# A cross-attention step with its two halves exchanged: values first, then the keys of one step further ahead

## The chip, the cores and the metric

The kernel runs on one core of a Trainium2 chip. The metric is the device time of one execution in microseconds (us), here the median of the runs of the kernel. A profiled execution gives the trace from which the rows below are read.

## The reference, cut to what matters

The program is one layer of a perceiver: cross-attention of 128 latent rows to a context of 12544 rows, then linear attention, causal attention and a mixture of eight experts on the 128 rows. Nearly all the time, and all of the change, is in the cross-attention:

```python
q = layernorm(x) @ Wq.T + bq                 # 128 x 256, 16 heads of 16
k = ctx @ Wk.T + bk                          # 12544 x 256
v = ctx @ Wv.T + bv                          # 12544 x 256
scores = einsum('bhqd,bhkd->bhqk', q * 0.25, k)
attn = softmax(scores, axis=-1)
x = x + einsum('bhqk,bhkd->bhqd', attn, v).reshape(...) @ Wo.T + bo
```

All of it is float32. The kernel keeps the accuracy by splitting operands into a high part and a low part in a float32r form and multiplying three of the four combinations.

## The kernel before, in words

**Tiling.** The 12544 context rows are cut into 49 pieces (`NS`) of 256 rows (`SK`). Four pieces make a block (`BS`), so there are 13 blocks. The program is a loop over steps t = 0 to 55. In one step, different pieces are at different stages:

- piece t+2: its keys (`keys`, 12 matmuls into `k_bank`, PSUM bank 0) and its values (`values`, 12 matmuls into `v_bank`, bank 1);
- piece t: the running maxima (`max_scores`: 16 matmuls, read by VectorE's `step_max`);
- piece n = t - 5 (`LAG`): the scores (`scores`, 16 matmuls, with the block's maxima subtracted by two extra rows of the query matrix `qmat`) and their exponentials on ScalarE (`exponential`);
- piece n - 1: the weighted values, a burst of 64 short matmuls (`weighted_values`, L605 in the trace) that accumulate in `pv_bank`.

**A step.** A step has eight slots, q = 0 to 7. In each slot TensorE does two matmuls of scores (L589), two of maxima (L565) and three of keys or values: keys (L533) in slots 0 to 3, values (L548) in slots 4 to 7. The burst comes at the end of slot 1. The maxima go to two banks in turn, so `max_scores` of a slot waits until VectorE has read that of two slots earlier (`mx_read`).

**Key parts.** Keys leave PSUM twice: ScalarE writes the high part to `kst` with the bias added (`keys_high`, L371, two instructions), VectorE the low part (`keys_low`, L901, two instructions). Before the change ScalarE does so after the exponential of slot 4 and VectorE after the maximum of slot 5. Then SyncE issues six DMAs (`keys_place`, L242) that copy `kst` to `kT`, a ring of 7 pieces, in the layout that the scores need. SyncE waits for three things before them: the low parts, a POOL memset of the ring slot (only for the first seven pieces), and the scores of the piece whose ring slot is overwritten. That is piece n-7, whose scores are done at the end of step n-2, the step in which the parts of piece n leave PSUM. TensorE waits for the six DMAs of piece t at the start of step t (`keys_placed`).

**Values out.** The values leave PSUM in one copy (`values_out`), by ScalarE for the first pieces and by VectorE (L911) from piece 6 on, in slot 1 of the following step.

**Context parts.** ScalarE makes the high part of the context of piece t+3 in slot 1 (`context_high`, L361), POOL then makes the low part (`context_low`, L314), both into a ring of two buffers, `cparts`. `ctx_load` on SyncE fetches the context of piece t+6 at the start of step t.

**Turned maxima.** After the last step of a block (in step last+1), VectorE reduces the maxima of four pieces (`block_max`, L925 to L935), TensorE turns them by a transpose in slot 2 (`turn_max`, L574, into `v_bank`), VectorE copies the result (`max_turned`, L942) and SyncE sends it to `qmat` by two DMAs (`max_rows`, L255). The scores of that block start at step last+2 and wait for these DMAs.

**Before and after the loop.** Ahead of step 0 come the keys and values of pieces 0 and 1. Steps 0 to 4 have no scores and no burst. From step 47 on there are no keys and no values, from step 49 on no maxima.

All order is written out by hand: each engine runs its own list, and semaphores connect them. There is no planner.

Of the kernel before, what the change touches and what calls it, by code (L numbers as in the profile page):

```python
# [6 lines left out]
F32R = mybir.dt.float32r  # L7
# [5 lines left out]
P = 128  # L13
# [8 lines left out]
NS = KEYS // SK  # L22
BS = 4
NB = (NS + BS - 1) // BS
LAG = BS + 1
# [31 lines left out]
def last_step(b):  # L57
    return min(b * BS + BS, NS) - 1
# [46 lines left out]
def perceiver_layer(nc, dr, out):  # L105
    ctx = ExitStack()
    with ctx:
# [3 lines left out]
        S = {n: ctx.enter_context(nc.semaphore(n)) for n in COUNTING + ONCE + LOADS + ["dve_chain"]}  # L111
# [18 lines left out]
        maxparts = sb("maxparts", [P, 8, 2, PAIRS], F32R)  # L130
        maxT = sb("maxT", [32, P], F32R)
# [223 lines left out]
        def _(act):  # L355
            def context_high(n):

                act.wait_ge(S[f"ld_ctx{n % CRING}"], 16 * (n // CRING) + 16)
                if n >= 2:
                    act.wait_ge(S["v_done"], 2 * (n - 2) + 2)  # L360
                act.activation(cparts[n % 2][:, 0, :, :], ctxT[n % CRING][:, :, :], ACT.Copy  # L361
                               ).then_inc(S["ch_ready"], 1)
# [12 lines left out]
            def values_out(n):  # L375


                act.wait_ge(S["v_done"], 2 * n + 2)
                if n >= VRING:
                    act.wait_ge(S["pv_done"], 2 * (n - VRING) + 2)  # L380
                act.activation(val[:, n % VRING, :, :, 0:HD].rearrange("p j h d -> p (j h) d"),  # L381
                               v_bank[:, :].rearrange("p (g d) -> p g d", d=HD), ACT.Copy).then_inc(S["val_ready"], 1)
# [32 lines left out]
            last.then_inc(S["act_q0"], 1)  # L415
            values_out(0)
            context_high(2)
            for t in range(LAST + 2):
                for q in range(8):
                    n = t - LAG  # L420
                    if 0 <= n < NS:
                        exponential(n, q)
                    if q == 1 and 0 <= t + 1 <= LAG:
                        values_out(t + 1)
                    if q == 1 and t + 3 < NS:
                        context_high(t + 3)
                    if q == 2:
                        for b in range(NB):
                            if n - 1 == last_step(b):
                                part_out(b)  # L430
                    if q == 4 and t + 2 < NS:
                        keys_high(t + 2)
                    if t == NS + 1 and q == 2:

                        act.wait_ge(S["dve_dmax"], 1)
                        act.activation(bmax[:, :, :], bmax[:, :, :], ACT.Exp).then_inc(S["act_bw"], 1)
# [71 lines left out]
        def _(pe):  # L508
# [16 lines left out]
            def keys(n, t, half):  # L525

                if (t, half) == (0, 0):
                    pe.wait_ge(S["cl_ready"], n + 1)
                    if n == 1:
                        pe.wait_ge(S["kl_ready"], 1)  # L530
                for i in range(3 * half, 3 * half + 3):
                    pw, pc, c = products[i]
                    last = pe.matmul(k_bank[:, t * SK:(t + 1) * SK], wk[:, pw, c, t * P:(t + 1) * P], cparts[n % 2][:, pc, c, :],  # L533
                                     start=(i == 0), stop=(i == 5))
                if (t, half) == (1, 1):
                    last.then_inc(S["k_done"], 1)

            def values(n, j, half):

                if (j, half) == (0, 0) and n >= 1:  # L540
                    turned = [b for b in range(NB) if last_step(b) == n - 3]
                    if turned:
                        pe.wait_ge(S["mt_read"], turned[0] + 1)
                    else:
                        pe.wait_ge(S["val_ready"], n)
                for i in range(3 * half, 3 * half + 3):
                    pw, pc, c = products[i]
                    last = pe.matmul(v_bank[:, j * D:(j + 1) * D], cparts[n % 2][:, pc, c, j * P:(j + 1) * P], wv[:, pw, c, :],  # L548
                                     start=(i == 0), stop=(i == 5))
                if half == 1:  # L550
                    last.then_inc(S["v_done"], 1)
# [5 lines left out]
            def max_scores(n, p):  # L557

                m = 8 * n + p
                if m >= 2:  # L560
                    pe.wait_ge(S["mx_read"], m - 1)
                for a in range(2):
                    if p == 0 and a == 1 and 0 < n + 2 < NS:
                        pe.wait_ge(S["kl_ready"], n + 2)
                    last = pe.matmul(mx_bank[p % 2][:, a * SK:(a + 1) * SK], qM[:, p, a, :], kT[:, n % RING, p, :],  # L565
                                     start=True, stop=True)
                last.then_inc(S["mx_done"], 1)

            def turn_max(b):


                pe.wait_ge(S["mparts_ready"], 2 * b + 2)
                pe.wait_ge(S["val_ready"], min(last_step(b) + 3, NS))
                pe.transpose(v_bank[:, 0:P].bitcast(F32R), maxparts[:, :, :, :].rearrange("q a s p -> q (a s p)"),  # L574
                             ident_r[:, :]).then_inc(S["mt_done"], 1)

            def scores(n, q):
# [37 lines left out]
            def turn_part(b):  # L615

                pe.wait_ge(S["part_ready"], b + 1)
                if b == 0:
                    pe.wait_ge(S["ld_small"], 64)
                    pe.wait_ge(S["kl_ready"], NS)  # L620
                if b == 1:
                    pe.wait_ge(S["mt_read"], NB)
                if b >= 2:
                    pe.wait_ge(S["dve_partT_read"], b - 1)
                for g in range(GROUPS):
                    last = pe.matmul(B[b % 2][:, g * GH * VW:(g + 1) * GH * VW], parts[:, b, g * P:(g + 1) * P],  # L626
                                     const[:, C_SEL:C_SEL + GH * VW], start=True, stop=True)
                last.then_inc(S["pe_partT"], 1)
# [32 lines left out]
            for n in range(2):  # L661
                for j in range(2):
                    for half in range(2):
                        values(n, j, half)
            pe.wait_ge(S["dve_q0"], 1)
            pe.wait_ge(S["act_q0"], 1)
            for t in range(LAST + 2):
                n = t - LAG
                for q in range(8):
                    if q == 0 and n < 0:  # L670
                        keys_placed(t)
                    if 0 <= n < NS:
                        scores(n, q)
                    if t < NS:
                        max_scores(t, q)
                    if q == 2:
                        for b in range(NB):
                            if t == last_step(b) + 1:
                                turn_max(b)
                    if t + 2 < NS:  # L680
                        if q < 4:
                            keys(t + 2, q // 2, q % 2)
                        else:
                            values(t + 2, (q - 4) // 2, q % 2)
                    if q == 1 and 0 <= n - 1:
                        weighted_values(n - 1, 0)
                        weighted_values(n - 1, 1)
                    if t > NS and q % 4 == 3 and 2 * (t - NS - 1) + q // 4 < NB - 3:
                        turn_part(2 * (t - NS - 1) + q // 4)
            for b in range(NB - 3, NB):  # L690
                turn_part(b)
# [155 lines left out]
        def _(dve):  # L847
# [89 lines left out]
            def max_turned(b):  # L937

                dve.wait_ge(S["mt_done"], b + 1)
                if b >= 1:  # L940
                    dve.wait_ge(S["max_rows"], 32 * b)
                dve.tensor_copy(maxT[:, :], v_bank[0:32, 0:P]).then_inc(S["mt_read"], 1)  # L942


            dve.memset(warm[:, :], 0.0).then_inc(S["dve_warm"], 1)
# [27 lines left out]
            for t in range(LAST + 2):  # L973
                for b in range(NB):
                    if t == last_step(b) + 1:
                        block_max(b)
                for q in range(8):
                    if t < NS:
                        step_max(t, q)
                    if q == 1 and LAG < t + 1 < NS:  # L980
                        values_out(t + 1)
                    if q == 2:
                        for b in range(NB):
                            if t == last_step(b) + 1:
                                max_turned(b)
                    if q == 5 and t + 2 < NS:
                        keys_low(t + 2)


            dve.wait_ge(S["ld_small"], 64)  # L990
# [283 lines left out]
```

## Time and profile before

| | us |
|---|---|
| median of 3 runs | 589.88 |
| lowest, highest | 588.37, 593.8 |
| the profiled execution | 590.74 |
| span of its trace | 588.9 |
| PE busy in the span | 555.1 (94%) |
| DVE busy | 423.2 (72%) |
| ACT busy | 331.6 (56%) |
| DMA queue q1, share of 16 engines | 64.1% |

A row of the trace names a line of the kernel, an engine and an operation. PE is a matmul on TensorE, PEld a weight load, DVE VectorE, ACT ScalarE, POOL GpSimd, SPq the DMA issue of SyncE. Matmuls overlap each other, so that their own durations are longer than the distance from one to the next; the chain of work shows that distance. The granted clock (PEclk) is a share of full speed: 1.00 is 2.4 GHz, 0.50 is 1.2 GHz.

### The profile page before, as it was taken

The numbers are of one execution on the slowest core, as the hardware profiler recorded it, in microseconds if no ns is written. First come the engines' busy times: TensorE is split into PE (matmuls) and PEld (weight loads), VectorE is DVE, ScalarE is ACT, GpSimd is POOL, SyncE is SP. The second block draws the span as 40 slices with busy tenths as digits, with TensorE's granted clock in tenths as the row PEclk, the third lists the DMA queues.
The fourth block names the chain that finished last, engine by engine and source line by source line (L and its number), as shares of the span: only waits on it lengthen the run. The fifth ranks groups of instructions, "written<-read, shape, count | busy, mean of one in ns | idle before, by whom it ended". The sixth has DMA issues, their size and how long they took to land.

```text
span 588.9 us, 15872 instructions
## 1 busy us (share of the span) xinstructions
PE 555.1 (94%) x6517; PEld 512.9 (87%) x6517; DVE 423.2 (72%) x804; ACT 331.6 (56%) x636; POOL 91.5 (16%) x75
## 2 busy tenths in 40 slices
PE   7778999999999999999999999999998998878797
PEld 7677899999999999999999999999986887846686
DVE  5678787787787787777787877877875237876674
ACT  3322666576676676676666666766766650052463
POOL 7551111111101101101101111011000000006000
PEclk9888999999999999999999999999999999988899
DMA  5999887768768778768678687785375009920000
GB/s 183 135 144 143 144 192 114 126 119 120 121 118 124 117 116 127 117 111 128 119 113 128 118 117 120 118 126 98 78 110 170 3 27 376 375 82 1 1 0 9
DMA packets 44651, 70.46 MB, mean 120 GB/s; under 512 B 6788, under 2 KB 15140, under 8 KB 44452
## 3 DMA queue, kind: packets, MB, share of 16 engines
q1 hardware_dynamic: 44580, 69.47, 64.1%
q8 instruction: 50, 0.82, 0.8%
q14 instruction: 21, 0.17, 0.1%
HBM read 30.56 MB, written 0.13 MB: 52 GB/s over the span
## 4 chain that ended last, share of the span: by engine, by line
PE 79%; DVE 7%; DMA 7%; SPq 3%; ACT 2%; issue 2%; DVEq 0%; ACTq 0%
PE bank L589 16%; PE bank L605 15%; PE bank L565 15%; PE bank L533 11%; PE bank L548 10%; DMA kT<-kst 5%; PE bank L805 3%; SPq L242 3%; PE bank L821 2%; PE bank L613 1%; DMA ctxT<-in_ctxT 1%; PE bank L626 1%; DVE stepmax L917 1%; DMA qmat<-maxT 1%; PE bank L518 1%
## 5 line engine op out<-in xcount | busy, mean ns | idle before, releaser
L917 DVE TENSOR_REDUCE stepmax<-bank 128x2 f32<-128x512 f32 x392 | 263.4, 688 | 98.8 <-PE bank L565 76.3
L391 ACT ACTIVATE probs<-bank 128x512 f32<-128x512 f32 x392 | 226.9, 602 | 146.3 <-PE bank L589 144.9
L565 PE MATMUL bank<-kT,qM 128*128 128x256 f32 x784 | 166.3, 294 | 8.5 <-DMA kT<-kst 7.1
L589 PE MATMUL bank<-qmat,kT 128*128 128x256 f32 x784 | 162.8, 292 | 4.3 <-DMA kT<-kst 1.7
L589 PEld LDWEIGHTS bank<-qmat,kT 128*128 128x128 f32 x784 | 120.2, 191 | 17.6 <-issue 10.1
L565 PEld LDWEIGHTS bank<-kT,qM 128*128 128x128 f32 x784 | 123.0, 194 | 14.2 <-DMA kT<-kst 7.0
L314 POOL TENSOR_TENSOR cparts<-ctxT,cparts 128x512 fp32r<-128x512 f32 x49 | 62.7, 1279 | 338.4 <-ACT cparts L361 338.4
L533 PE MATMUL bank<-cparts,wk 128*128 128x256 f32 x588 | 104.2, 288 | 1.9 <-DVE kst L901 1.9
L548 PE MATMUL bank<-wv,cparts 128*128 128x256 f32 x588 | 101.9, 284 | 0.7 <-ACT val L381 0.7
L605 PE MATMUL bank<-probs,val 128*17 128x128 f32 x3136 | 95.1, 273 | 0.0
L533 PEld LDWEIGHTS bank<-cparts,wk 128*128 128x128 f32 x588 | 86.2, 196 | 2.3 <-POOL cparts L314 2.3
L605 PEld LDWEIGHTS bank<-probs,val 128*17 128x17 f32 x3136 | 81.4, 97 | 6.5
L548 PEld LDWEIGHTS bank<-wv,cparts 128*128 128x128 f32 x588 | 84.6, 193 | 0.9 <-ACT val L381 0.9
L371 ACT ACTIVATE kst<-bank,kbias 128x256 fp32r<-128x256 f32 x98 | 40.9, 472 | 22.1 <-PE bank L533 22.1
L901 DVE SCALAR_TENSOR_TENSOR kst<-bank,kbias,kst 128x256 fp32r<-128x256 f32 x98 | 42.5, 475 | 4.1 <-ACT kst L371 4.1
L361 ACT ACTIVATE cparts<-ctxT 128x512 fp32r<-128x512 f32 x49 | 30.5, 623 | 3.5 <-DMA ctxT<-in_ctxT 3.5
L911 DVE COPY val<-bank 128x512 f32<-128x512 f32 x43 | 29.2, 680 | 0.0
L350 POOL TENSOR_TENSOR low<-w,high 128x512 fp32r<-128x512 f32 x8 | 10.1, 1303 | 109.7 <-ACT high L462 109.7
L805 PE MATMUL bank<-high,tparts 128*128 128x512 f32 x64 | 20.2, 439 | 0.2 <-DVE tparts L1142 0.2
L1181 DVE TENSOR_TENSOR low<-w,high 128x1024 f32 (+1 forms) x12 | 14.7, 1222 | 6.0 <-ACT high L462 6.0
L613 PE MATMUL bank<-const 128*128 128x128 f32 x136 | 18.9, 285 | 0.0
L613 PEld LDWEIGHTS bank<-const 128*128 128x128 f32 x136 | 17.8, 201 | 0.3
(188 smaller groups left out, 324.9 us busy)
## 6 DMA issues: line engine op xcount, KB each, us to landing
kT<-kst SPq DMA_DIRECT2D x294, 128.0 KB, 4.6
ctxT<-in_ctxT SPq DMA_DIRECT2D x49, 256.0 KB, 5.3
w<-in_w SPq DMA_DIRECT2D x24, 512.0 KB, 10.1
bias<-in_biases SPq DMA_DIRECT2D x1, 1024.0 KB, 5.9
qmat<-maxT SPq DMA_DIRECT2D x26, 8.0 KB
w_xk<-in_w_xk SPq DMA_DIRECT2D x1, 256.0 KB, 3.4
w_xq<-in_w_xq SPq DMA_DIRECT2D x1, 256.0 KB, 3.5
bias<-in_biases SPq DMA_DIRECT2D x1, 256.0 KB, 6.0
```

The lines of the kernel that those rows point to most:

```text
L314: pool.tensor_tensor(cparts[n % 2][:, 1, :, :], ctxT[n % CRING][:, :, :], cparts[n % 2][:, 0, :, :].bitcast(F32), ALU.subtract).then_inc(S ...
L371: last = act.activation(kst[n % 2][:, 0, t * SK:(t + 1) * SK], k_bank[:, t * SK:(t + 1) * SK], ACT.Identity, bias=kbias[:, t:t + 1])
L391: act.activation(probs[k % PROBS][:, :, :], sc_bank[k % 3][:, :].rearrange("p (h q) -> p h q", q=P), ACT.Exp).then_inc(S["exp_ready"], 1)
L533: last = pe.matmul(k_bank[:, t * SK:(t + 1) * SK], wk[:, pw, c, t * P:(t + 1) * P], cparts[n % 2][:, pc, c, :], start=(i == 0), stop=(i == 5))
L548: last = pe.matmul(v_bank[:, j * D:(j + 1) * D], cparts[n % 2][:, pc, c, j * P:(j + 1) * P], wv[:, pw, c, :], start=(i == 0), stop=(i == 5))
L565: last = pe.matmul(mx_bank[p % 2][:, a * SK:(a + 1) * SK], qM[:, p, a, :], kT[:, n % RING, p, :], start=True, stop=True)
L589: last = pe.matmul(sc_bank[k % 3][:, i * 2 * P:(i + 1) * 2 * P], kT[:, n % RING, p, j * P:(j + 1) * P], qmat[b % 2][:, p, :, :], start=Tru ...
L605: last = pe.matmul(pv_bank[32 * r:32 * r + VW, g * P:(g + 1) * P], val[:, n % VRING, j, GH * g + r, :], probs[(GROUPS * ch + g) % PROBS][: ...
L613: pe.matmul(B[6][:, 0:P], ident, ident, start=True, stop=True)
L805: last = pe.matmul(B[2 * which + i][:, :], tparts[:, a, c, :], weights, start=(n == 0), stop=(n == len(products) - 1))
L901: last = dve.scalar_tensor_tensor(kst[n % 2][:, 1, cols], k_bank[:, cols], kbias[:, t:t + 1], kst[n % 2][:, 0, cols].bitcast(F32), ALU.add ...
L917: dve.tensor_reduce(stepmax[:, n % BS, 2 * p:2 * p + 2], mx_bank[p % 2][:, :].rearrange("p (a k) -> p a k", a=2), AX_X, ALU.max).then_inc( ...
```

## The change

The two halves of a step are exchanged. Values of piece t+2 are computed in slots 0 to 3, and keys of piece t+3 (not t+2) in slots 4 to 7. The keys of piece 2 move ahead of the loop. The key parts of piece t+2, whose matmuls now lie in the step before, leave PSUM in step t in slot 0 on ScalarE and slot 1 on VectorE, beside the burst. The values leave in slot 5 of the same step instead of slot 1 of the next. The context's high part is made in slot 5, of piece t+4. The turned maxima use `k_bank` instead of `v_bank`, because that bank is now the one that is empty in slot 2. The waits follow: TensorE's wait for the context parts moves to slot 2, the wait for the key parts to slot 4, and the wait for the values out of PSUM to slot 0. No instruction that computes or copies is added or taken away, and the ring sizes stay.

```diff
@@ ScalarE: before the loop, and in the loop
             values_out(0)
             context_high(2)
+            values_out(1)
+            context_high(3)
             for t in range(LAST + 2):
                 for q in range(8):
                     n = t - LAG
                     if 0 <= n < NS:
                         exponential(n, q)
-                    if q == 1 and 0 <= t + 1 <= LAG:
-                        values_out(t + 1)
-                    if q == 1 and t + 3 < NS:
-                        context_high(t + 3)
+                    if q == 0 and t + 2 < NS:
+                        keys_high(t + 2)
+                    if q == 5 and t + 2 <= LAG:
+                        values_out(t + 2)
+                    if q == 5 and t + 4 < NS:
+                        context_high(t + 4)
...
-                    if q == 4 and t + 2 < NS:
-                        keys_high(t + 2)
@@ TensorE: keys, values, max_scores, turn_max, turn_part
             def keys(n, t, half):
 
                 if (t, half) == (0, 0):
-                    pe.wait_ge(S["cl_ready"], n + 1)
-                    if n == 1:
-                        pe.wait_ge(S["kl_ready"], 1)
+                    if n < 3:
+                        pe.wait_ge(S["cl_ready"], n + 1)
+                    if n >= 1:
+                        turned = [b for b in range(NB) if last_step(b) == n - 4]
+                        if turned:
+                            pe.wait_ge(S["mt_read"], turned[0] + 1)
+                        else:
+                            pe.wait_ge(S["kl_ready"], n)
...
                 if (j, half) == (0, 0) and n >= 1:
-                    turned = [b for b in range(NB) if last_step(b) == n - 3]
-                    if turned:
-                        pe.wait_ge(S["mt_read"], turned[0] + 1)
-                    else:
-                        pe.wait_ge(S["val_ready"], n)
+                    pe.wait_ge(S["val_ready"], n)
...
-                    if p == 0 and a == 1 and 0 < n + 2 < NS:
-                        pe.wait_ge(S["kl_ready"], n + 2)
+                    if p == 2 and a == 1 and n + 3 < NS:
+                        pe.wait_ge(S["cl_ready"], n + 4)
...
                 pe.wait_ge(S["mparts_ready"], 2 * b + 2)
-                pe.wait_ge(S["val_ready"], min(last_step(b) + 3, NS))
-                pe.transpose(v_bank[:, 0:P].bitcast(F32R), maxparts[:, :, :, :].rearrange("q a s p -> q (a s p)"),
+                pe.wait_ge(S["kl_ready"], min(last_step(b) + 4, NS))
+                pe.transpose(k_bank[:, 0:P].bitcast(F32R), maxparts[:, :, :, :].rearrange("q a s p -> q (a s p)"),
@@ TensorE: before the loop, and in the loop
+            for t in range(2):
+                for half in range(2):
+                    keys(2, t, half)
...
-                    if t + 2 < NS:
-                        if q < 4:
-                            keys(t + 2, q // 2, q % 2)
-                        else:
-                            values(t + 2, (q - 4) // 2, q % 2)
+                    if q < 4 and t + 2 < NS:
+                        values(t + 2, q // 2, q % 2)
+                    if q >= 4 and t + 3 < NS:
+                        keys(t + 3, (q - 4) // 2, q % 2)
@@ VectorE: max_turned, and in the loop
-                dve.tensor_copy(maxT[:, :], v_bank[0:32, 0:P]).then_inc(S["mt_read"], 1)
+                dve.tensor_copy(maxT[:, :], k_bank[0:32, 0:P]).then_inc(S["mt_read"], 1)
...
-                    if q == 1 and LAG < t + 1 < NS:
-                        values_out(t + 1)
+                    if q == 1 and t + 2 < NS:
+                        keys_low(t + 2)
...
-                    if q == 5 and t + 2 < NS:
-                        keys_low(t + 2)
+                    if q == 5 and LAG < t + 2 < NS:
+                        values_out(t + 2)
```

**VectorE's list around a block's end.** The names: `stepmax` is the maximum of one slot, `kst` the low key parts, `val` the copy of the values, `curmax` to `bmax` the block's maxima, `maxT` the copy of the turned ones. Before:

```order
L917 TENSOR_REDUCE stepmax<-bank 128x2 x4
L901 SCALAR_TENSOR_TENSOR kst_75<-bank,kbias,kst_75 128x256 x2
L917 TENSOR_REDUCE stepmax<-bank 128x2 x2
L925 TENSOR_REDUCE curmax<-stepmax 128x16
L931 TENSOR_SCALAR maxparts<-curmax 128x2x8
L933 SCALAR_TENSOR_TENSOR maxparts<-curmax,maxparts 128x2x8
L935 TENSOR_SCALAR bmax<-curmax 128x16
L917 TENSOR_REDUCE stepmax<-bank 128x2 x2
L911 COPY val<-bank 128x32x16
L917 TENSOR_REDUCE stepmax<-bank 128x2
L942 CAST maxT<-bank 32x128
L917 TENSOR_REDUCE stepmax<-bank 128x2 x3
```

With the change:

```order
L923 TENSOR_REDUCE stepmax<-bank 128x2 x4
L917 COPY val<-bank 128x32x16
L923 TENSOR_REDUCE stepmax<-bank 128x2 x2
L931 TENSOR_REDUCE curmax<-stepmax 128x16
L937 TENSOR_SCALAR maxparts<-curmax 128x2x8
L939 SCALAR_TENSOR_TENSOR maxparts<-curmax,maxparts 128x2x8
L941 TENSOR_SCALAR bmax<-curmax 128x16
L923 TENSOR_REDUCE stepmax<-bank 128x2 x2
L907 SCALAR_TENSOR_TENSOR kst_74<-bank,kbias,kst_74 128x256 x2
L923 TENSOR_REDUCE stepmax<-bank 128x2
L948 CAST maxT<-bank 32x128
L923 TENSOR_REDUCE stepmax<-bank 128x2 x3
```

The two key instructions and the one value copy have changed places: the copy stands after slot 5 and the keys after slot 1.

**TensorE's list from slot 7 of a step over slots 0 and 1 of the next.** `qmat,kT` are scores, `kT,qM` maxima, `cparts,wk` keys, `wv,cparts` values; in brackets are the semaphores waited for. Before:

```order
L548 MATMUL bank<-wv,cparts_70 128x256 x3
L589 MATMUL bank<-qmat_51,kT 128x256 [waits exp_ready]
L589 MATMUL bank<-qmat_51,kT 128x256 [waits kt_load1]
L565 MATMUL bank<-kT,qM 128x256 [waits mx_read]
L565 MATMUL bank<-kT,qM 128x256 [waits kl_ready]
L533 MATMUL bank<-cparts_71,wk 128x256 [waits cl_ready]
L533 MATMUL bank<-cparts_71,wk 128x256 x2
```

With the change:

```order
L540 MATMUL bank<-cparts_71,wk 128x256 x3
L592 MATMUL bank<-qmat_51,kT 128x256 [waits exp_ready]
L592 MATMUL bank<-qmat_51,kT 128x256 [waits kt_load1]
L568 MATMUL bank<-kT,qM 128x256 [waits mx_read]
L568 MATMUL bank<-kT,qM 128x256
L551 MATMUL bank<-wv,cparts_71 128x256 [waits val_ready]
L551 MATMUL bank<-wv,cparts_71 128x256 x2
```

Slot 0 now has values where it had keys, and one wait less; the wait for `mx_read` in front of the maxima is unchanged.

## Rows read from the trace of the kernel before

**Rows 1.** Page: engines' shares of the chain that ended last.

```profile
PE 79%; DVE 7%; DMA 7%; SPq 3%; ACT 2%; issue 2%; DVEq 0%; ACTq 0%
```

**Rows 2.** Chain of waits, slots 7 to 1 of a middle step: start us, us, what.

```profile
239.04 1.87 PE bank L605 x64
...
246.14 0.24 PE bank L589 x2
246.38 0.39 PE bank L565 x2
246.77 0.36 PE bank L533 x3
...
247.37 0.24 PE bank L565 x2
...
247.96 1.87 PE bank L605 x64
```

**Rows 3.** Timeline of the same place: start, us, engine, line, operation.

```profile
244.75 0.87 DVE L901 SCALAR_TENSOR_TENSOR kst<-bank,kbias,kst 128x256 fp32r<-128x256 f32 x2
...
245.53 2.81 DVE L917 TENSOR_REDUCE stepmax<-bank 128x2 f32<-128x512 f32 x4
...
245.64 3.77 SPq L242 DMA_DIRECT2D kT<-kst  x6
...
246.26 0.50 PE L565 MATMUL bank<-kT,qM 128*128 128x256 f32 x2
...
248.25 0.68 DVE L911 COPY val<-bank 128x512 f32<-128x512 f32 x1
```

**Rows 4.** Chain of waits from step 0 to step 6.

```profile
22.02 0.47 PE bank L565 x2
...
27.70 0.79 DVE kst L901 x2
28.51 0.55 SPq L242
...
31.67 5.23 DMA kT<-kst
...
36.94 0.80 PE bank L565 x2
...
67.15 0.38 PE bank L589
```

**Rows 5.** Timeline around the starts of steps 0, 1 and 5; in brackets idle time before.

```profile
22.02 0.47 PE L565 MATMUL bank<-kT,qM 128*128 128x256 f32 x2 [2.14 <-DMA kT<-kst]
...
28.40 5.20 DVE L917 TENSOR_REDUCE stepmax<-bank 128x2 f32<-128x512 f32 x8
...
29.23 0.47 PE L565 MATMUL bank<-kT,qM 128*128 128x256 f32 x2 [0.62 <-DVE stepmax L917]
...
29.84 1.29 POOL L314 TENSOR_TENSOR cparts<-ctxT,cparts 128x512 fp32r<-128x512 f32 x1 [3.26 <-ACT cparts L361]
...
59.62 0.50 PE L589 MATMUL bank<-qmat,kT 128*128 128x256 f32 x2 [0.85 <-DMA qmat<-maxT]
```

**Rows 6.** Stretches: us, busy (x) of PE PEld DVE ACT POOL, PEclk, DMA share, GB/s.

```profile
24.00:26.00 2.00, 2.00 (x11) 2.00 (x10) 1.30 (x2) 0.00 (x0) 2.00 (x2) 0.50 1.09 137
...
28.00:30.00 2.00, 1.38 (x12) 1.21 (x11) 1.94 (x5) 1.12 (x2) 0.16 (x1) 1.00 0.12 40
30.00:43.00 13.00, 10.57 (x74) 10.26 (x73) 10.05 (x18) 2.80 (x6) 7.72 (x5) 0.87 1.05 148
```

**Rows 7.** `stepmax` instructions while a POOL instruction on the context runs: count, duration ns min/median/max.

```profile
L917 DVE TENSOR_REDUCE stepmax<-bank x3: 681/690/691, 29.7 to 31.0; 128x2 f32<-128x512 f32 x3
```

**Rows 8.** Chain of waits, steps 46 to 48.

```profile
433.08 0.79 DVE kst L901 x2
...
437.05 5.65 DMA kT<-kst
```

**Rows 9.** Chain of waits at the start of step 37.

```profile
341.59 3.22 DMA qmat<-maxT
```

More of the change, by code:

```diff
@@ L620, in turn_part @@
                     pe.wait_ge(S["kl_ready"], NS)
+                    pe.wait_ge(S["mt_read"], NB)
                 if b == 1:
-                    pe.wait_ge(S["mt_read"], NB)
+                    pe.wait_ge(S["val_ready"], NS)
                 if b >= 2:
```

## The prediction

> **What bounds the kernel now.** I read the page first: 79% of the chain that ended last is TensorE, and DMA only 7% [rows 1]. The chain in order of time then shows two regimes. In the middle it is TensorE without a gap that the page counts as idle. From one burst to the next are 247.96 - 239.04 = 8.92 us [rows 2], and steps 6 to 46 all look like that. Two matmuls take 0.24 us there, three take 0.36. Only one place in a step is longer for no visible reason: the two maxima of slot 0 take 0.39 where those of slot 1 take 0.24. The timeline explains it [rows 3]. VectorE starts the low key parts at 244.75, after the maximum of slot 5, and needs 0.87. The maximum of slot 6 can start only at 245.53 and, at 0.69 us, is read by 246.22. TensorE's slot 0 of the next step writes the same bank, and it starts at 246.26, right behind that. Without the extra 0.15 of the chain (0.39 against 0.24) it would have started at about 246.11. So 0.15 us of each step is a wait for VectorE that is too short to appear as idle time.
>
> In the start-up it is different. From step 0 at 22.02 to step 6 at 67.15 two steps take about 15 us (the first two 36.94 - 22.02 = 14.9, [rows 4]), though TensorE's 40 matmuls of a step need 40 x 0.12 = 4.8 us. The loop that sets this pace is: start of step t, key parts in slots 4 and 5 (27.70 + 0.79), six DMA issues from 28.51 on [rows 4], the last landing at 31.67 + 5.23 = 36.90, start of step t+2.
>
> **The change, part by part.** The sum is made against the profiled execution, 590.74 us, which is 0.86 above the median of the three runs.
>
> *Steady steps.* VectorE's work per step is the same: eight maxima, 0.87 of keys, 0.68 of values [rows 3]. The keys now follow slot 1, where VectorE waits for TensorE through the 1.87 us of the burst [rows 2]; 0.87 fits and costs nothing. Before, the values' 0.68 stood there. The values now follow slot 5. There they delay the maximum of slot 6 by 0.68 where the keys did so by 0.87, so it is read 0.19 earlier, at 246.03 in the times of rows 3. TensorE's own pace asks for 246.11, so the stall of 0.15 goes, with some 0.04 to spare after the 0.04 of signalling. What is late next is nothing on VectorE: slot 7 follows by 0.69 where TensorE allows 0.84. I found the same 0.39 in some 30 of the 40 steps 7 to 46 and 0.27 to 0.36 in those next to a block's end, so 30 x 0.15 + 10 x 0.09 = **5.4 us**.
>
> ScalarE and POOL only change the hour. The high key parts (ScalarE, slot 0) delay the exponential of slot 1, which the burst hides; without the burst it would be 0.8 us against 0.24 us of spare per slot. The context goes high and low in slots 5 to 7, two slots or more ahead of TensorE's wait in slot 2. SyncE's six key DMAs of a middle step are issued at 245.64, the moment the low parts are done, but they also wait for the scores of slot 7, which end within 0.2 us of that. So earlier key parts do not make these DMAs earlier: no gain, no loss. Moving waits on TensorE costs nothing either: the three keys of slot 0 stand behind a wait for `cl_ready` and take 0.36 [rows 2], like any other three.
>
> *Start-up.* With the keys of piece 2 ahead of the loop, the low parts leave after two maxima, about 2.8 us into step 0, not at 27.70 (5.7 in). The 12 matmuls moved ahead, 1.4 us, fall in TensorE's wait of 2.14 us for the first DMAs [rows 5]: nothing. The latency loop becomes 2.8, six issues of 3.8 in all [rows 3] and a landing of 5.2 [rows 4], 11.8 us for two steps. Two other things are slower than that. VectorE needs 5.20 for eight maxima [rows 5] and 0.87, so 6.1 a step. The DMA engines are full: 13 us with a share of 1.05 carried two steps' keys and contexts [rows 6], so 6.5 a step. Step 1 starts at 29.23 as before [rows 5], since its keys are untouched; step 6 then starts at 29.2 + 5 x 6.5 = 61.7 by DMA. By VectorE it is 29.5 + 5 x 6.1 plus block 0's reduction (0.7), its copy (0.3) and two value copies (1.4) = 62.4. Before it was 67.15. So at most 4.8 is gained. Against it stand step 5's wait for the turned maxima of block 0, queued behind a full set of key DMAs (59.62, [rows 5]), and TensorE's clock, granted at 0.50 after each long wait [rows 6]. Steps of 7.0 instead of 6.5 would leave 2. I take **4.0 us**, nearer the upper end, because the waits that lower the clock get shorter.
>
> *End.* Step 46 has only values now: 12 x 0.12 = 1.44 us less. The keys of piece 48 wait for the end of that step's scores as much as for their own low parts (433.08 + 0.79), and step 48 starts when they land at 437.05 + 5.65 = 442.7 [rows 8]. All of that moves ahead by 1.44. Step 47 may now wait up to 1 us for piece 47, but piece 48's DMAs do not wait for it. I take **1.4 us**.
>
> *Turned maxima.* TensorE's transpose at a block's end needs the low key parts out of `k_bank`. VectorE starts the block's reduction about 0.9 us into the step and needs 0.7 for it, 1.3 for two maxima and 0.87 for the keys, 3.8 in all; the transpose comes after three slots and the burst, 3 x 0.84 + 1.87 = 4.4. So 0.6 is to spare, where the values had 0.8. The DMAs that follow it landed too late for the next block once, at the start of step 37 (341.59 + 3.22, some 0.35 late) [rows 9]. With 0.15 less between the key DMAs and this one it may happen once more: **-0.3 us**.
>
> Sum: 5.4 + 4.0 + 1.4 - 0.3 = 10.5. 590.74 - 10.5 = 580.2, and 589.88 - 10.5 = **579.4 us** for the median.
>
> **The rivals.**
>
> *The stall in slot 0 stays (13%).* For it: my spare is 0.04 us, and slot 0 still has three waits on TensorE, so the 0.15 could belong to them rather than to VectorE. Against: TensorE's start is behind VectorE's end by 0.04 in every step that I looked at, and waits elsewhere cost nothing. Then only start-up and end gain: 589.88 - 5.1 = 584.8.
>
> *The maxima's DMAs are late at each block (8%).* Ten block ends lie in the steady part. If each costs the 0.35 of step 37, the sum falls by 3.2 more: 582.6.
>
> *POOL and VectorE collide (4%).* POOL's 1.3 us on the context [rows 5] used to run during the burst. Now it runs under the maxima of slots 6 and 7, where only 0.04 us is to spare. If a maximum had to wait for it, every step would lose up to 1.2, and 40 x 1.2 - 5.1 makes 633; the point from which the kernel is slower than before is a delay of 0.04 of spare, 0.15 and 5.1 / 40, together 0.32 us per step. Against it: three maxima took 681 to 691 ns while such a POOL instruction ran in step 1 [rows 5, 7], and 0.69 is also the time of one without it. The Trainium skill (SBUF — State Buffer, the section on the two sides of the memory) says that POOL and VectorE take an exclusive lock on a shared port pair when a VectorE instruction runs in a two-port mode or has two SBUF inputs, and that the loser waits for the whole instruction. By that rule a maximum, which reads PSUM, is not affected, and the trace agrees.
>
> *The exchange does not reach the start-up (5%).* If the full DMA engines already set the pace there, so that steps stay at 7.5, only 7 is left: 583.
>
> **How the numbers follow.** The forecast has 70%; its own range is 577.5 (start-up 4.8, stall 5.8, end 1.7) to 582.5 (start-up 2, stall 4.5, end 1). The rivals at 582.6 to 584.8 have 26%. The range 576.5 to 585 holds these less their outermost part. What a measurement of this kernel can tell from no change is about 1%, 5.9 us, so the line is at 584.0: faster by over 1% has 0.82 (the forecast, the two rivals below 584, less mishaps), within 1% 0.14, slower 0.04.
>
> **What would show it.** In the chain of a middle step the maxima of slot 0 take 0.24 and bursts are 8.78 apart. Step 6 starts near 63 and the share of DMA is above 1 through all of 30 to 60 us. Step 48 starts about 10.5 us earlier than at 442.7. I am wrong if the maxima of slot 0 stay at 0.39, if `stepmax` lasts over 0.7 us beside POOL, or if TensorE's idle time in front of L589 grows by releases from `maxT`.

## The result, and the profile after

The changed kernel takes 582.55 us in the median of 4 runs (581.65 to 583.93); the kernel before took 591.84 beside it (4 runs, 588.37 to 594.27). The ratio is 0.987, with a 95% interval of 0.982 to 0.991: 1.3% faster. In a second comparison, in 6 runs against 11, the same kernel gave 582.46 and a ratio of 0.983 (0.978 to 0.988). The forecast was 579.4 with a range of 576.5 to 585.0, and a gain of 10.5; by the two profiled executions the span shrank by 588.9 - 580.6 = 8.3.

The page of the changed kernel, against [rows 1]: the span, the granted clock in 40 slices, and the engines' shares of the chain.

```profile
span 580.6 us, 15874 instructions
...
PEclk9999999999999999999999999999999999988899
DMA  6999996766877877876768768777483029900000
...
PE 78%; DVE 10%; DMA 6%; SPq 3%; ACT 2%; issue 1%; DVEq 0%; ACTq 0%
```

**A middle step.** The chain of waits of the changed kernel, from slot 7 to the next burst, against [rows 2] (L568 are the maxima, L608 the burst). The maxima of slot 0, at 240.47, now take 0.24 like all others, and bursts are 8.78 apart.

```profile
239.63 0.24 PE bank L568 x2
240.47 0.24 PE bank L568 x2
241.31 0.24 PE bank L568 x2
241.91 1.87 PE bank L608 x64
...
250.69 1.87 PE bank L608 x64
```

The timeline of the same place, against [rows 3]: the values' copy stands where the keys stood, and it lets the next maximum start 0.60 later, where the keys took 0.78. POOL's context work now runs beside the maxima.

```profile
247.62 0.68 DVE L917 COPY val<-bank 128x512 f32<-128x512 f32 x1
247.96 1.29 POOL L314 TENSOR_TENSOR cparts<-ctxT,cparts 128x512 fp32r<-128x512 f32 x1 [7.49 <-ACT cparts L361]
248.22 0.68 DVE L923 TENSOR_REDUCE stepmax<-bank 128x2 f32<-128x512 f32 x1
```

How far TensorE had to wait is best seen on its weight loads (PEld), since the wait for the bank holds back the load of the maxima's weights too, and such a load runs 0.12 ahead of its matmul when nothing holds it (248.97 and 249.09 with the change). Before, the loads of scores and maxima at the start of slot 0, which stand 0.40 apart:

```profile
245.86 0.31 PEld L589 LDWEIGHTS bank<-qmat,kT 128*128 128x128 f32 x2
246.26 0.30 PEld L565 LDWEIGHTS bank<-kT,qM 128*128 128x128 f32 x2
```

With the change they stand 0.24 apart, as in every other slot, though only just: the maximum that frees the bank ends at 248.22 + 0.68 = 248.90, and the kernel before needed 0.05 from such an end (245.53 + 0.68 = 246.21) to the load at 246.26. That leaves 0.02.

```profile
248.73 0.31 PEld L592 LDWEIGHTS bank<-qmat,kT 128*128 128x128 f32 x2
248.97 0.31 PEld L568 LDWEIGHTS bank<-kT,qM 128*128 128x128 f32 x2
```

All `stepmax` instructions of 100 to 400 us, against [rows 7] (count, duration ns min/median/max): none is lengthened by POOL.

```profile
L923 DVE TENSOR_REDUCE stepmax<-bank x271: 678/691/693, 100.1 to 399.2; 128x2 f32<-128x512 f32 x136
```

**The start-up.** The chain of the changed kernel from step 1 to step 6, against [rows 4]. Step 1 starts at 28.20, step 3 at 41.16 (6.5 a step), step 6 at 61.52 instead of 67.15. From 43.77 to 54.60 the chain is nearly all VectorE; before it was six issues and a landing in each round. From 30.84 to 41.12 it still is, but the landing takes 7.12 instead of 5.23.

```profile
28.20 0.52 PE bank L568 x2
...
30.03 0.79 DVE kst L907 x2
...
34.00 7.12 DMA kT<-kst
...
41.16 0.52 PE bank L568 x2
...
42.99 0.78 DVE kst L907 x2
43.77 3.78 DVE stepmax L923 x6
...
49.54 0.79 DVE kst L907 x2
...
61.52 0.47 PE bank L592 x2
```

Two stretches of it (us, busy (x) of PE, PEld, DVE, ACT, POOL, PEclk, DMA share, GB/s), against [rows 6]. The clock stays at 1.00 where before it fell to 0.50 after each long wait, and the DMA engines have a mean share of 1.07 from 14 to 52 us, with no 2 us below 1.01. The prediction's sign, a share above 1 through all of 30 to 60 us, holds only to 52: from 52 to 62 it is 0.79.

```profile
30.00:43.00 13.00, 11.01 (x82) 10.06 (x82) 11.73 (x22) 3.91 (x8) 5.02 (x4) 1.00 1.07 164
14.00:52.00 38.00, 31.06 (x229) 28.28 (x230) 30.56 (x57) 12.95 (x27) 18.30 (x12) 1.00 1.07 158
```

**Step 8.** In the changed kernel one step has a wait that the kernel before does not have. The chain there: the six key DMAs of piece 8 are issued from 70.03 on, right behind 1.3 MB of biases and constants, and the last needs 7.73 us to land.

```profile
70.03 0.55 SPq L242
...
73.20 7.73 DMA kT<-kst
80.97 0.39 PE bank L592
```

**The end.** The chain of the changed kernel in step 46, against [rows 8]. Without keys in slots 4 to 7, TensorE waits for a maximum (422.96), and the scores of slot 7 release the DMA issue.

```profile
422.69 0.25 PE bank L568 x2
422.96 0.70 DVE stepmax L923
423.71 0.51 PE bank L568 x2
424.22 0.25 PE bank L592 x2
424.48 0.03 SPq L238
424.54 0.55 SPq L242
...
427.69 5.66 DMA kT<-kst
433.40 0.38 PE bank L592
```

The starts of the bursts (L605 before, L608 after), read from the timelines, make the account:

| burst of step | before | after | ahead by |
|---|---|---|---|
| 6 | 68.89 | 63.35 | 5.54 |
| 7 | 77.81 | 72.14 | 5.67 |
| 8 | 86.73 | 82.72 | 4.01 |
| 46 | 427.22 | 418.63 | 8.59 |
| 49 | 450.73 | 441.37 | 9.36 |
| 54, the last | 481.15 | 471.81 | 9.34 |
| end of the span | 588.9 | 580.6 | 8.3 |

Not all of this is the change. `e0_after` below is the changed kernel once more, and its bursts of steps 6 and 54 come 0.9 later than in the first profile. Nearly all of that is there already when step 0 starts, which moves with the first loads:

| profile | step 0 starts | last burst | between |
|---|---|---|---|
| kernel before | 22.02 | 481.15 | 459.13 |
| changed | 21.36 | 471.81 | 450.45 |
| `e0_after` | 22.34 | 472.74 | 450.40 |

In the seven other experiments step 0 starts at 21.50 to 22.47. So 0.66 of each line of the account lies in front of step 0 and is no gain that the change is shown to make; from step 0 to the last burst it makes 8.7.

### The profile page after: what moved, and what is told of

It is laid out like the page before. It is cut to its first block, busy times and chain, and to the rows that moved or that the text cites. A ratio compares the mean times of both kernels' runs of the same rounds, so it can differ in the third digit from the quotient of the medians.

```text
span 580.6 us, 15874 instructions
## 1 busy us (share of the span) xinstructions
PE 548.3 (94%) x6517; PEld 507.2 (87%) x6517; DVE 421.7 (73%) x804; ACT 331.4 (57%) x636; POOL 91.8 (16%) x75
## 4 chain that ended last, share of the span: by engine, by line
PE 78%; DVE 10%; DMA 6%; SPq 3%; ACT 2%; issue 1%; DVEq 0%; ACTq 0%
PE bank L592 17%; PE bank L608 15%; PE bank L568 14%; PE bank L551 10%; PE bank L540 10%; DMA kT<-kst 5%; PE bank L811 3%; PE bank L827 3%; SPq L242 2%; DVE stepmax L923 2%; PE bank L616 1%; PE bank L630 1%; DMA ctxT<-in_ctxT 1%; PE bank L520 1%; DVE kst L907 1%
## 5 line engine op out<-in xcount | busy, mean ns | idle before, releaser
L391 ACT ACTIVATE probs<-bank 128x512 f32<-128x512 f32 x392 | 230.8, 599 | 141.9 <-PE bank L592 137.5
L568 PE MATMUL bank<-kT,qM 128*128 128x256 f32 x784 | 161.1, 287 | 4.9 <-DMA kT<-kst 2.6
L568 PEld LDWEIGHTS bank<-kT,qM 128*128 128x128 f32 x784 | 121.4, 191 | 8.9 <-DVE stepmax L923 4.5
L540 PE MATMUL bank<-cparts,wk 128*128 128x256 f32 x588 | 101.1, 283 | 1.6 <-DVE kst L907 1.3
L608 PE MATMUL bank<-probs,val 128*17 128x128 f32 x3136 | 95.1, 273 | 0.0
L608 PEld LDWEIGHTS bank<-probs,val 128*17 128x17 f32 x3136 | 81.4, 97 | 6.5
L540 PEld LDWEIGHTS bank<-cparts,wk 128*128 128x128 f32 x588 | 83.8, 192 | 2.3 <-POOL cparts L314 2.1
```

Source lines behind the costliest of these rows:

```text
L391: act.activation(probs[k % PROBS][:, :, :], sc_bank[k % 3][:, :].rearrange("p (h q) -> p h q", q=P), ACT.Exp).then_inc(S["exp_ready"], 1)
L608: last = pe.matmul(pv_bank[32 * r:32 * r + VW, g * P:(g + 1) * P], val[:, n % VRING, j, GH * g + r, :], probs[(GROUPS * ch + g) % PROBS][: ...
```

## The experiments

Each was compared with the kernel before on the same chip. Since the part behind the last burst varies by itself (below), I read single terms from the bursts of the profiled execution.

**Is the stall of slot 0 VectorE's backlog?** Two experiments, one from each side. `e1_split` takes the kernel before and parts the low keys:

```diff
                     if q == 5 and t + 2 < NS:
-                        keys_low(t + 2)
+                        keys_low(t + 2, (0,))
+                    if q == 6 and t + 2 < NS:
+                        keys_low(t + 2, (1,))
```

(`keys_low` is given the halves that it shall do, and signals after the second.)

> The kernel before, with VectorE's two low-part instructions parted: one after slot 5, one after slot 6. Theory V (the 0.15 us of slot 0 is VectorE's backlog of 0.87 us on the maximum of slot 6): that maximum is now late by 0.43 only, so the maxima of slot 0 fall from 0.39 to 0.24; the maximum of slot 7 is late by both, so slot 1 should rise from 0.24 to about 0.30, and bursts be some 8.85 apart instead of 8.92. The start-up loop gets 0.7 longer each time, three times, step 6 near 69; the whole about 589 to 591 where before gives 591. Theory W (the 0.15 belongs to TensorE's three waits in slot 0): slot 0 stays at 0.39 and bursts at 8.92.

Measured: undisturbed bursts are 8.80 apart; slot 0 takes 0.27 instead of 0.39, and slot 1 stays at 0.24, not the 0.30 that I expected. Two rows of its chain, slots 0 and 1:

```profile
251.50 0.27 PE bank L565 x2
...
252.36 0.24 PE bank L565 x2
```

So theory V holds, and W falls: the three waits are all still there. But the kernel as a whole took 598.25, ratio 1.011 (1.004 to 1.019), some 7 us more than I expected. The timeline shows why:

```profile
250.85 0.47 DVE L901 SCALAR_TENSOR_TENSOR kst<-bank,kbias,kst 128x256 fp32r<-128x256 f32 x1
251.25 2.08 DVE L918 TENSOR_REDUCE stepmax<-bank 128x2 f32<-128x512 f32 x3
...
251.34 0.43 PE L565 MATMUL bank<-kT,qM 128*128 128x256 f32 x2
251.35 3.76 SPq L242 DMA_DIRECT2D kT<-kst  x6
```

The key DMAs start together with slot 0's maxima of the next step, where in the kernel before they start 0.6 ahead of them (245.64 against 246.26, [rows 3]). What SyncE issues behind them is late too, and the first steps of the blocks, steps 13 to 41, take 9.36 to 9.86 instead of 9.03 (9.39 once): eight waits for the turned maxima. The two waits for keys in the rows below are at step 8 (2.2) and in one middle step. The idle time in front of L589 from 68 to 430 us:

```profile
PE bank L589 <- DMA qmat<-maxT: 3.4, 8, 0.7
PE bank L589 <- DMA kT<-kst: 2.4, 2, 2.2
```

By the last burst (489.39 against 481.15) the loss is 8.2: 1.7 in the start-up, where I expected about 2, 2.2 in steps 7 and 8, 2.4 net in the steady part, and 1.9 in steps 47 to 49. That all of it comes from the later key DMAs is read from the timeline and was not tested by itself. The kernel before stood at two limits, with 0.15 to gain on one and hardly anything to give on the other.

`e2_dose` takes the changed kernel and lengthens the backlog after slot 5 with an instruction of no use:

```diff
                     if q == 5 and LAG < t + 2 < NS:
                         values_out(t + 2)
+                        dve.memset(small[:, 224:480], 0.0)
```

> The changed kernel, with one more VectorE instruction after the copy of the values in slot 5: it fills 256 unused columns and should take 0.2 to 0.33 us, so that the backlog on slot 6 is as large as the 0.87 of before or larger. Theory V: the wait comes back in slot 0, about this instruction's time less 0.06, so bursts are 8.92 to 9.05 apart instead of 8.78, and the kernel loses 40 times that, 6 to 11 us. Theory W: nothing moves, 582.5.

Measured: bursts 8.955 apart, and slot 0 at 0.43. The next maximum starts 251.28 - 250.41 = 0.87 behind the values' copy, where it was 0.60; it is 0.05 shorter than there, so it frees the bank 0.22 later. The loads of TensorE's maxima stand 0.44 behind those of the scores (251.53).

```profile
250.41 0.68 DVE L917 COPY val<-bank 128x512 f32<-128x512 f32 x1
251.10 0.27 DVE L994 MEMSET small<- 128x256 f32 x1
251.28 0.63 DVE L923 TENSOR_REDUCE stepmax<-bank 128x2 f32<-128x512 f32 x1
251.97 0.30 PEld L568 LDWEIGHTS bank<-kT,qM 128*128 128x128 f32 x2
```

A bank freed 0.22 later costs 8.955 - 8.78 = 0.175 a step: the spare is the rest, 0.05 at most, and the 0.04 of the forecast is of the right size. The last burst is 5.8 us later than in the changed kernel, of which 1.1 is a later start of step 0 (22.47). The other 4.6 are less than 40 x 0.175 = 7, because the longer step swallows all but one of the eight waits at block ends and most of that of step 8 (9.32 instead of 10.58). The whole took 586.23, ratio 0.990 (0.981 to 0.998). Theory V again.

**What sets the pace of the start-up now?** `e3_late` holds the key parts back by two slots there:

```diff
-                    if q == 0 and t + 2 < NS:
+                    if q == (2 if t < LAG else 0) and t + 2 < NS:
                         keys_high(t + 2)
...
-                    if q == 1 and t + 2 < NS:
+                    if q == (3 if t < BS else 1) and t + 2 < NS:
                         keys_low(t + 2)
```

> The changed kernel, where in the start-up the key parts leave PSUM two slots later (ScalarE slot 2, VectorE slot 3). Theory D (after the change the DMA engines, at a share of 1.07, and VectorE set the start-up's pace, not the latency of the loop): step 6 starts at most 1 us later than its 61.5. Theory L (the loop of key parts, issue and landing still sets it): each of three rounds of two steps is 1.3 longer, step 6 at 65.4, the kernel 3.9 slower.

Measured: the burst of step 6 at 64.47, 1.1 later than 63.35, where theory L asked for 3.9. Of the 1.1, 0.4 lies ahead of step 0, which starts at 21.79, so that the edit costs 0.7. The DMA share of 30 to 43 us fell from 1.07 to 0.97, with one hole of some size (0.58 from 40 to 42 us). Theory D. The burst of step 8 comes at 82.93 against 82.72, so that even this is nearly gone two steps later; the kernel takes 582.57.

**Who holds step 8?** `e4_biases` moves the load of biases and constants from step 5 to the end:

```diff
-                if t == LAG:
-                    sp.dma_start(biases[:, early:], dr["biases"][early:].partition_broadcast(P)).then_inc(S["ld_small"], 16)
+                if t in (NS - 6, NS - 5):
+                    half = early + (t - NS + 6) * 4 * D
+                    sp.dma_start(biases[:, half:half + 4 * D], dr["biases"][half:half + 4 * D].partition_broadcast(P)
+                                 ).then_inc(S["ld_small"], 16)
+                if t == NS - 4:
```

(and the two waits for `ld_small` count 80 instead of 64).

> The changed kernel, where the loads of the biases and constants (1.3 MB, after step 5's key DMAs) move to steps 43 to 45, in which no context is fetched, the biases in two halves. Theory B (step 8's wait of 1.7 us for its keys, which the kernel before does not have, comes from these loads in front of them): it goes, bursts 7 and 8 are 8.8 apart instead of 10.6, and the kernel is 1 to 1.7 us faster unless steps 44 to 46 now wait. Other theory (it is left over from the full queue of the start-up): it stays at least in half.

Measured: bursts 7 and 8 are 8.78 apart instead of 10.58. Theory B. Step 45 now takes 9.62 instead of 8.89, because a half of the biases lies in front of turned maxima. The last burst comes at 471.09 against 471.81, 0.7 ahead and not 1 to 1.7. The kernel took 582.10 (5 runs), which can't be told from the changed one.

**Does the end of the program vary by itself?** `e0_after` is the changed kernel, unchanged.

> The changed kernel once more, for the same chip as the next three: steady bursts 8.78 apart, step 8 late by 1.8, the first steps of blocks 8.88 to 9.18 apart. The part behind the last burst took 107.8 us before, 108.8 with the change and 105.0 with the biases moved, in profiles whose granted clock there differs. If that is chance of the execution (theory C), this profile's part behind the last burst may be any of 105 to 109 though nothing is changed; if it belongs to the kernel (theory K), it is 108.8 again.

Measured: the part behind the last burst took 582.5 - 472.74 = 109.8 us, against 108.8 in the first profile of the same kernel, a little outside the 105 to 109 that I had allowed, and its six runs lie between 577.5 and 585.39. The two fastest have a mean clock of 0.994, the slowest 0.982; but a run of 582.45 has 0.982 as well. Stretches of 25 us, from 35 us behind the last burst, in the kernel before, the changed one, `e0_after` and `e4_biases` show where:

```profile
516.15:541.15 25.00, 19.59 (x113) 13.91 (x114) 16.54 (x40) 10.62 (x27) 10.06 (x8) 0.80 0.12 37
```

```profile
506.81:531.81 25.00, 18.41 (x109) 13.55 (x110) 15.81 (x36) 10.62 (x27) 10.04 (x8) 0.80 0.11 34
```

```profile
506.80:531.80 25.00, 18.15 (x99) 13.25 (x100) 15.12 (x32) 10.62 (x27) 9.52 (x8) 0.73 0.15 48
```

```profile
506.09:531.09 25.00, 18.96 (x114) 12.87 (x115) 18.11 (x45) 10.62 (x27) 10.06 (x8) 0.88 0.11 34
```

In this stretch of small dependent stages the clock is granted at half for a part that differs from run to run: 0.73 goes with 109.8 us, 0.80 with 107.8 and 108.8, 0.88 with 105.0. The mean alone doesn't explain the 1.0 us that the first pair of profiles loses, since it is 0.80 in both. What work the half clock falls on does. VectorE's instructions start within 0.04 us of each other, counted from the last burst, up to 34 us behind it. From 34 to 44 us the granted clock is 0.83 before and 1.00 with the change, and the changed kernel gains 0.65; from 44 to 57 us it is 0.74 and 0.61, among denser matmuls, and it loses more than that. Theory C, then, for the variation. That the first pair's 1.0 us is pure chance is not shown: the profiles of `e2_dose`, `e3_late` and `e7_all` have the same 108.7 to 108.8 behind the last burst, while all profiles of the changed order go from 105.0 to 110.3.

**What do the turned maxima wait for?** `e5_ctx` changes SyncE's order at a block's end:

```diff
-                if CRING <= t + 6 < NS:
+                ends = [b for b in range(NB) if t == last_step(b) + 1]
+                if not ends and CRING <= t + 6 < NS:
+                    ctx_load(t + 6)
+                for b in ends:
+                    max_rows(b)
+                if ends and CRING <= t + 6 < NS:
                     ctx_load(t + 6)
-                for b in range(NB):
-                    if t == last_step(b) + 1:
-                        max_rows(b)
```

> The changed kernel, where SyncE at a block's end sends the turned maxima first and fetches the context after them. Theory Q (the maxima's two DMAs queue behind 256 KB of context, so that the next block's first scores wait 0 to 0.3 us at each of ten blocks): the first steps of blocks are 8.89 apart everywhere (8.78 and the 0.11 of the transpose), 1.2 us less in all. Other theory (they wait for VectorE's copy): as before, 8.88 to 9.18.

Measured: all first steps of blocks, 13 to 45, take 8.89; with the change alone they take 8.89 to 9.18. Summed over steps 8 to 46 this is 334.70 instead of 335.91. Theory Q, and the size to 0.1 us. SyncE's issues at step 12, of the changed kernel and then of this one:

```profile
121.08 0.59 SPq L230 DMA_DIRECT2D ctxT<-in_ctxT  x1
121.78 1.34 SPq L255 DMA_DIRECT2D qmat<-maxT  x2
124.71 4.91 SPq L242 DMA_DIRECT2D kT<-kst  x6
```

```profile
121.31 1.34 SPq L255 DMA_DIRECT2D qmat<-maxT  x2
122.69 0.39 SPq L230 DMA_DIRECT2D ctxT<-in_ctxT  x1
124.52 4.20 SPq L242 DMA_DIRECT2D kT<-kst  x4
```

By the whole time (one run, 582.52) it cannot be seen.

**The last maxima.** `e6_tail` is a miss:

```diff
-                if t == NS - 2:
+                if t == NS:
 
                     sp.wait_ge(S["v_done"], 2 * NS)
                     for name in WEIGHTS[3:]:
                         sp.dma_start(*weight(name)).then_inc(S["ld_tail"], 16)
```

> The changed kernel, where the ten weight loads of the next stages (2.6 MB) come after the last turned maxima instead of ahead of the last two. If the maxima's DMAs of block 11 wait behind these loads, step 49 is 5.9 instead of 6.95 long: 1.0 us less, and nothing lost later, since the first of these weights is needed 40 us on. If they do not, 6.95 stays.

Measured: step 49 takes 6.88 instead of 6.95. Its maxima wait for no other load: their two DMAs need 1.92 us after the last issue with the loads gone (1.98 with them), and in the chain they follow VectorE's copy and the issue. Step 48 was 0.5 shorter here (7.36), but not in the next kernel, which has the same move; I leave that open. The one run of the whole took 581.58.

**All three.** `e7_all` joins the moves of loads, the biases in quarters in the place of a context load:

> The three moves of loads together, the biases now in quarters in steps 43 to 46 in the place of a context load, the constants at step 47. Sum: step 8's 1.8, the blocks' 1.2 and step 49's 1.0 make 4.0 us by the last burst (467.8 instead of 471.8). By the whole time 578.5 against 582.5 if the part behind it takes the same; it may hide or double this, by 3 us either way.

Measured: last burst at 469.09 instead of 471.81, and 580.06 us in the median of 6 runs, ratio 0.980 (0.976 to 0.984), beside 0.983 (0.978 to 0.988) of the changed kernel in the same rounds. By the bursts it is 2.7 us faster, not 4.0: step 8 (1.7) and the blocks (1.0, since step 45 still waits 0.2) came, step 49 did not. By the medians, 580.06 against 582.46, it is the fastest of the kernels, but their intervals overlap.

## Why the prediction was right

**Steady steps (5.4 forecast, with -0.3 for the maxima).** Bursts 8.78 apart, and the extra 0.15 of slot 0 gone, as forecast. From step 8 to 46 the changed kernel gains 8.59 - 4.01 = 4.58 in 38 steps, where the sum has 5.1 for 40. The cause stood two tests: less backlog in the old order removes the stall, more of it in the new order brings it back. The values' 0.68 is just short enough: the margin that I gave as 0.04 is 0.02 by the weight loads and at most 0.05 by `e2_dose`. The waits at block ends cost 1.2 in the changed kernel, as `e5_ctx` shows, where the kernel before had 0.36 in one step; so they took 0.8 from the gain and not 0.3.

**Start-up (4.0, at most 4.8).** By the burst of step 6 it was 5.5, but 0.66 of that is the earlier start of step 0, which `e0_after` doesn't repeat; counted from step 0 it was 4.9 in both profiles of the changed kernel, still past my upper end. Two reasons could have been read from the rows. Step 1 was not untouched: it had waited 0.62 for VectorE [rows 5], whose keys of slot 5 are gone, and starts 6.84 after step 0 instead of 7.21. And the clock, which I charged with part of 0.8, stays at 1.00 through the whole start-up. The latency of the loop no longer sets the pace, as forecast (`e3_late`); which of DMA and VectorE does, no run separates. But 1.5 is given back by step 8, and this I had not seen: I had noted neither the 1.3 MB of step 5 nor that they come in the same queue between the keys of pieces 7 and 8. In the kernel before they were hidden. What is left is 3.4, so 4.0 came out nearly right by luck: two errors of opposite sign.

**End (1.4).** The failed step: "all of that moves ahead by 1.44". The gain from step 46 to 49 is 9.36 - 8.59 = 0.77. I had taken away TensorE's 12 matmuls and not asked what is next: without them a slot takes 0.48 on TensorE and 0.69 on VectorE, and VectorE sets the second half of the step. Step 48 starts at 433.40 instead of 442.74, 9.3 earlier and not 10.5.

**Rivals.** The stall that stays and the collision of POOL with VectorE did not happen; 271 maxima between 678 and 693 ns, beside POOL's work in every step, agree with the rule of the Trainium skill that I had quoted (SBUF — State Buffer, the section on the two sides), by which a VectorE instruction takes the shared ports only in a two-port mode or with two SBUF inputs. The late maxima happened at 0.12 a block instead of 0.35. The exchange did reach the start-up.

**The sum.** Counted from step 0 to the last burst the change gives 8.7 of the 10.5: 3.4 up to step 8, 4.6 in the steady part, 0.8 at the end, each a little under its term. The profiles add 0.66 in front of step 0 and take 1.0 behind the last burst, which makes 8.3 by the spans; the medians, 591.84 and 582.55, are 9.3 apart. That the time came within 3.2 us of the forecast thus rests on the right mechanism in the steady steps, and in the start-up partly on luck. The forecast's own range of 577.5 to 582.5 is also summed without the 0.3 for the maxima; with it, it is about 577.9 to 582.7.

## What to carry to other kernels

A wait shorter than the overlap of two matmuls is in no idle column, here 0.15 us in each of some 30 steps. It shows as a stretch of the chain that is longer in one slot than in the others, and as a longer distance between weight loads; the engine to look at is the one that frees the bank. Extra work of an engine that runs just behind the bound belongs where the bound does something that does not need it, here the burst. And when a phase gets shorter, list what its queues carry besides: what was hidden in the slack of the old pace is charged at the first place where the new pace meets it. Count every profile from a common event, here the start of step 0, before you split a difference into terms: the kernel's own start moved by 1 us between executions.

## What the hardware showed that I had not expected

- The same kernel took 577.5 to 585.39 us. The mean clock is 0.994 in its two fastest executions and 0.982 in its slowest; in profiles of the changed order the part behind the last burst took 105.0 to 110.3 us, and step 0 started at 21.36 to 22.47. A difference of 1 to 3 us has to be read from the trace between these two points.
- Starting six DMAs 0.6 us later in a step of 8.9 went with a loss of 1% (`e1_split`), though the DMA engines had a share of only 0.74 in the middle of the kernel before (104 to 140 us).
- A wait of TensorE for a PSUM bank holds the weight load in front of the matmul as well: the matmul started only 0.05 late (246.26 instead of 245.38 + 0.84), and the pair ended 0.15 late.
